# In every step of a local-attention stack, the order of two transposes on TensorE and of four pieces of work on ScalarE is changed

## The reference, cut to what matters

```
for i in range(DEPTH):                                # 6
    x = attn_layer(shift_tokens(x), Wqkv[i], q_scale[i], k_scale[i], Wo[i]) + x
    x = ffn_layer(shift_tokens(x), ln_g[i], ln_b[i], W1[i], b1[i], W2[i], b2[i]) + x

def attn_layer(x, Wqkv, qs, ksc, Wo):                 # HEADS 16, DIM_HEAD 64
    q, k, v = split(x @ Wqkv)
    q, k = l2norm(q) * qs, l2norm(k) * ksc            # needs the inverse lengths of q and k
    q, k = rotary(q), rotary(k)
    out = local_attention(q, k, v)                    # windows of 32 queries see 64 keys; softmax
    return out @ Wo
```

## Time and profile before

| | |
|---|---|
| Median of 3 runs | 4589.51 us (4580.05 to 4589.95) |
| The profiled execution | 4575.15 us |
| Its span, first to last instruction | 4573.3 us |
| Instructions | 164587 |
| TensorE busy | 4055.2 us, 89% |
| GpSimd busy | 3001.9 us, 66% |
| VectorE busy | 2776.7 us, 61% |
| ScalarE busy | 2723.2 us, 60% |

### The profile page before, as it was taken

One profiled execution on the slowest core, in us unless ns is written; L12 is line 12 of the kernel. 1 busy time (PEld: TensorE's weight loads), 2 busy tenths in 40 slices (PEclk: granted clock), 3 DMA queues, 4 the chain that ended last, 5 costly groups with the idle time before them and its releaser, 6 DMA issues.

```text
span 4573.3 us, 164587 instructions
## 1 busy us (share of the span) xinstructions
PE 4055.2 (89%) x67239; PEld 2824.1 (62%) x67239; DVE 2776.7 (61%) x4602; ACT 2723.2 (60%) x5657; POOL 3001.9 (66%) x1858
## 2 busy tenths in 40 slices
PE   8989999999999999967999999999999997276975
PEld 5656666666666666635666666666666663153654
DVE  5556666666666666635666666666666663624541
ACT  5656666666666666634666666666666664134752
POOL 0068888888888888815888888888888882511001
PEclk9999999999999999989999999999999998587997
DMA  2023333333333333312333343333333331030004
GB/s 68 2 65 88 102 98 92 102 91 102 99 92 103 90 101 100 92 39 50 95 99 97 89 107 94 97 98 89 106 94 98 98 89 32 0 111 14 2 11 122
DMA packets 349821, 367.95 MB, mean 80 GB/s; under 512 B 58737, under 2 KB 285042, under 8 KB 348786
## 3 DMA queue, kind: packets, MB, share of 16 engines
q1 hardware_dynamic: 338834, 348.92, 29.2%
q0 software_dynamic: 2048, 4.20, 0.3%
q10 hardware_dynamic: 8160, 3.93, 0.3%
HBM read 247.12 MB, written 109.71 MB: 78 GB/s over the span
## 4 chain that ended last, share of the span: by engine, by line
PE 35%; ACT 8%; issue 3%; POOL 2%; DVE 2%; SPq 1%; DMA 1%; ACTq 0%; POOLq 0%; DVEq 0%
PE banks L325 6%; PE banks L386 3%; PE banks L309 3%; PE banks L330 3%; PE banks L430 2%; PE banks L369 2%; PE banks L292 2%; PE banks L845 1%; PE banks L424 1%; PE banks L863 1%; ACT arena L461 1%; PE banks L880 1%; PE banks L1311 1%; PE banks L1331 1%; ACT ln_rs L467 1%
## 5 line engine op out<-in xcount | busy, mean ns | idle before, releaser
L637 POOL TENSOR_TENSOR arena<-arena 128x512 f32<-128x512 f32 x768 | 960.4, 1272 | 522.6 <-DVE arena L566 401.6
L642 POOL TENSOR_TENSOR arena<-arena 128x1024 f32<-128x1024 f32 x384 | 905.9, 2359 | 30.1
L639 POOL TENSOR_TENSOR arena<-arena 128x1024 f32<-128x1024 f32 x384 | 907.8, 2364 | 0.0
L325 PE MATMUL banks<-w_qk,arena 128*128 128x512 f32 x1536 | 735.7, 602 | 15.5 <-DVE arena L666 10.6
L440 ACT COPY arena<-banks 128x512 f32<-128x512 f32 x384 | 224.3, 584 | 806.1 <-PE banks L386 806.1
L566 DVE SCALAR_TENSOR_TENSOR arena<-arena,banks 128x512 f32<-128x512 f32 x768 | 493.3, 684 | 308.1 <-ACT arena L474 306.6
L559 DVE TENSOR_REDUCE arena<-arena 128x8 f32<-128x512 f32 x768 | 494.2, 679 | 86.4 <-ACT arena L456 86.4
L533 DVE TENSOR_REDUCE arena<-banks 128x8 f32<-128x512 f32 x384 | 264.7, 689 | 399.9 <-PE banks L309 396.2
L456 ACT ACTIVATE arena<-banks 128x512 f32<-128x512 f32 x768 | 447.8, 596 | 82.8 <-PE banks L325 71.0
L325 PEld LDWEIGHTS banks<-w_qk,arena 128*128 128x128 f32 x1536 | 277.0, 193 | 271.6 <-issue 271.6
L386 PE MATMUL banks<-ident,arena 128*128 128x128 f32 x3072 | 424.7, 282 | 20.0 <-POOL arena L642 19.4
(11 more groups left out here) (220 smaller groups left out, 6715.1 us busy)
## 6 DMA issues: line engine op xcount, KB each, us to landing
v_rows<-arena SPq DMA_DIRECT2D x1536, 64.0 KB
arena<-v_rows SPq DMA_DIRECT2D x768, 128.0 KB
arena<-v_rows SPq DMA_DIRECT2D x768, 112.0 KB
arena<-in_moe_w SPq DMA_DIRECT2D x30, 515.5 KB, 3.8
w_qk<-in_stack_qk SPq DMA_DIRECT2D x48, 256.0 KB, 3.1
w_v<-in_stack_v SPq DMA_DIRECT2D x48, 128.0 KB, 3.4
w_o<-in_stack_o SPq DMA_DIRECT2D x12, 512.0 KB
w_w<-in_stack_w SPq DMA_DIRECT2D x12, 341.0 KB, 3.2
```

What stands on the lines that cost most here:

```text
L325: pe.matmul(bank(M, tile), f.sh[:, (s // G) % 2, o:o + 128], w.qk[:, g], start=True, stop=True).then_inc(S.qk, 1)
L637: nc.gpsimd.tensor_tensor(f.sined[:, :, :, half, :], x[:, :, :, 1 - half, :], sines[:, :, mine].unsqueeze(1).to_broadcast([D, GH, 4, DH // ...
L639: nc.gpsimd.tensor_tensor(rot, x.rearrange("p h t a d -> p h t (a d)"), cosines.unsqueeze(1).to_broadcast([D, GH, 4, DH]), ALU.mult).then_ ...
L642: nc.gpsimd.tensor_tensor(rot, rot, f.sined.rearrange("p h t a d -> p h t (a d)"), ALU.add).then_inc(S.rotated, 1)
```

## The change

On TensorE the turning of the outputs, which stood behind the value projection and ahead of place 1, is moved behind place 1 and behind the turning of the probabilities. On ScalarE the order behind the values' copy was outputs' copy, inverse lengths (logarithm, exponential), place 1, probabilities' copy; now it is place 1, probabilities' copy, outputs' copy, inverse lengths, except in steps 3 and 7 (`s % G == 3`), where place 1 stays behind the inverse lengths. The number of instructions and their sizes stay.

```diff
@@ pe_stack_step
-    if st.on(4):
-        u = s - 4
-        st.wait(S.normed, u + 1)
-        st.wait(S.heads_taken, u + 3 if st.on(2) else u + 2 if st.on(3) else u + 1)
-        ...
-        last.then_inc(S.outs_turned, 1)
     pe_stack_hidden(M, st, 1)
-    if st.on(3):
-        ...
-        last.then_inc(S.probs_turned, 1)
+    pe_stack_probs_turned(M, st)
+    pe_stack_outs_turned(M, st)
     if st.on(4) and s % G == 3:
@@ pe_stack_outs_turned (new; holds what was removed above, and one wait for the tail)
+        if not st.on(2):
+            st.wait(S.outs_taken, u)
@@ act_stack_step
     nc.scalar.copy(f.vt[:, u % 2]...).then_inc(S.v_taken, 1)
-    if st.on(4):
-        u = s - 4
-        st.wait(S.outs_turned, u + 1)
-        ...
-        nc.scalar.copy(stack_hidden(M).ot[:, u % G]..., bank(M, 3)).then_inc(S.outs_taken, 1)
+    if s % G != 3:
+        act_stack_hidden(M, st, 1)
+    if st.on(3):
+        u = s - 3
+        st.wait(S.probs_turned, u + 1)
+        st.wait(S.outs, u)
+        nc.scalar.copy(f.pt..., bank(M, 6)).then_inc(S.probs_taken, 1)
+    act_stack_outs(M, st)
     if st.on(0):
         u = s
         st.wait(S.lengths, u + 1)
         nc.scalar.activation(f.lg, f.length, ACT.Ln).then_inc(S.logged, 1)
         ...
         nc.scalar.activation(f.rn[:, u % 2], f.lg, ACT.Exp, scale=-0.5).then_inc(S.inverse, 1)
-    act_stack_hidden(M, st, 1)
-    if st.on(3):
-        ...
-        nc.scalar.copy(f.pt..., bank(M, 6)).then_inc(S.probs_taken, 1)
+    if s % G == 3:
+        act_stack_hidden(M, st, 1)
     act_stack_hidden(M, st, 2)
```

More of the change, by code:

```diff
@@ L332, in pe_stack_step @@
         last.then_inc(S.v, 1)
-    if st.on(4):
-        u = s - 4
-        st.wait(S.normed, u + 1)
-        st.wait(S.heads_taken, u + 3 if st.on(2) else u + 2 if st.on(3) else u + 1)
[L337 to L341, removed]
-        last.then_inc(S.outs_turned, 1)
-    pe_stack_hidden(M, st, 1)
-    if st.on(3):
[L345 to L352, removed]
-        last.then_inc(S.probs_turned, 1)
+    pe_stack_hidden(M, st, 1)
+    pe_stack_probs_turned(M, st)
+    pe_stack_outs_turned(M, st)
     if st.on(4) and s % G == 3:
@@ L372, in pe_stack_step, with pe_stack_outs_turned, pe_stack_probs_turned @@
     pe_stack_hidden(M, st, 2)
+def pe_stack_outs_turned(M, st):
+    pe, s, S, f = st.eng, st.s, M.st, stack_buffers(M)
+    if st.on(4):
+        u = s - 4
+        st.wait(S.normed, u + 1)
+        st.wait(S.heads_taken, u + 3 if st.on(2) else u + 2 if st.on(3) else u + 1)
+        if not st.on(2):
+            st.wait(S.outs_taken, u)
+        ov = f.o.rearrange("p (t h) d -> p t h d", t=2)
+        for hp in range(2):
+            for tile in range(2):
+                last = pe.transpose(bank(M, 3)[:, hp * T + tile * 128:hp * T + tile * 128 + 128],
+                                    ov[:, tile, 2 * hp:2 * hp + 2, :], M.ident[:])
+        last.then_inc(S.outs_turned, 1)
+def pe_stack_probs_turned(M, st):
+    pe, s, S, f = st.eng, st.s, M.st, stack_buffers(M)
+    if st.on(3):
+        u = s - 3
+        st.wait(S.probs, u + 1)
+        st.wait(S.probs_taken, u)
+        pv = f.p.rearrange("p (t h) k -> p t h k", t=2)
+        for tile in range(2):
+            for hp in range(2):
+                o = (2 * tile + hp) * 128
+                last = pe.transpose(bank(M, 6)[:, o:o + 128], pv[:, tile, 2 * hp:2 * hp + 2, :], M.ident[:])
+        last.then_inc(S.probs_turned, 1)
 def pe_stack_heads(M, st, qk):
@@ L457, in act_stack_step @@
                                  ACT.Square).then_inc(S.squared, 1)
+    if st.on(0):
+        u = s
         st.wait(S.v, u + 1)
@@ L461, in act_stack_step @@
         nc.scalar.copy(f.vt[:, u % 2].rearrange("p t a c -> p (t a c)"), bank(M, 2)).then_inc(S.v_taken, 1)
-    if st.on(4):
-        u = s - 4
-        st.wait(S.outs_turned, u + 1)
-        if u % G == 0 and not (st.first and u == 0):
-            act.wait_ge(S.projected, st.f * 2 + u // G)
-        nc.scalar.copy(stack_hidden(M).ot[:, u % G].rearrange("p h t -> p (h t)"), bank(M, 3)).then_inc(S.outs_taken, 1)
+    if s % G != 3:
+        act_stack_hidden(M, st, 1)
+    if st.on(3):
+        u = s - 3
+        st.wait(S.probs_turned, u + 1)
+        st.wait(S.outs, u)
+        nc.scalar.copy(f.pt.rearrange("p t h k -> p (t h k)"), bank(M, 6)).then_inc(S.probs_taken, 1)
+    act_stack_outs(M, st)
     if st.on(0):
@@ L474, in act_stack_step, with act_stack_outs @@
         nc.scalar.activation(f.rn[:, u % 2], f.lg, ACT.Exp, scale=-0.5).then_inc(S.inverse, 1)
-    act_stack_hidden(M, st, 1)
-    if st.on(3):
[L477 to L480, removed]
-    act_stack_hidden(M, st, 2)
+    if s % G == 3:
+        act_stack_hidden(M, st, 1)
+    act_stack_hidden(M, st, 2)
+def act_stack_outs(M, st):
+    act, s, S, nc = st.eng, st.s, M.st, M.nc
+    if st.on(4):
+        u = s - 4
+        st.wait(S.outs_turned, u + 1)
+        if u % G == 0 and not (st.first and u == 0):
+            act.wait_ge(S.projected, st.f * 2 + u // G)
+        nc.scalar.copy(stack_hidden(M).ot[:, u % G].rearrange("p h t -> p (h t)"), bank(M, 3)).then_inc(S.outs_taken, 1)
 def act_stack_hidden(M, st, place):
```

## The result

The changed kernel takes 4635.4 us (median; 4634.11 to 4639.9) against 4588.4 us before, a ratio of 1.0107 with a 95% interval of 1.0092 to 1.0122. It is 47 us slower; 54 were forecast (4643, range 4608 to 4675).

What follows compares the result with a forecast made beforehand. TensorE was taken as the bound, its stops set by ScalarE's order. 36 pairs at +0.97 us and ten layer starts at +2.21 gave 57, taken as 54: 4589.5 + 54 = 4643.5, said as 4643 us, range 4608 to 4675.

Steps and rivals of the forecast that it cites:

- Part 1: Probabilities' copy first on ScalarE: shorter TensorE stops at L309 in steps 0, 5, 6 and at step 6's gate product, at most 1.93 us a pair.
- Step 6: L309's stop and part of the third gate product's wait go, 0.05 us charged for the rotation: -0.87 us.
- Part 2: Outputs' copy one copy later, so L369 waits longer in steps 3 and 7: 2 x 0.48 = 0.96 us a pair.
- Part 3: Inverse lengths (L474) last on ScalarE, delaying VectorE's L566 and the work behind it, and GpSimd's rotation; meets something in four places.
- Step 2 into 3: Inverse lengths delay the next scores' maximum by 1.1 to 1.2 us; about 0.45 reaches L369, ends 0 and 0.8.
- Steps 4 and 5: Inverse lengths 0.54 us late through a chain without slack to the variance, swallowing 0.38 won at L309: +0.54 us.
- Steps 0 and 1: Inverse lengths 1.13 us late stop step 1's value product, leaving 0.11 of L309's 0.63: -0.11 us, +1.13 at layer starts.
- The sum: All terms together: +0.97 us in a usual pair, +2.21 in one starting a later layer; 57 us, taken as 54.
- the late inverse lengths cost nothing: Rival: their delay is hidden in steps 0, 2 and 4, a gain of 0.97 us in 46 pairs, 4545 us; 5%.
- the sum would be nothing: Rival: step 2's delay dies out on the squares and layer starts cost no more than other pairs, near 4595 us; 5%.
- the gains don't come: Rival: L309 and the gate product find another late partner, up to 0.9 us more a pair, about 4680 us; 8%.
- the clock falls in every pair: Rival: longer stops before L369 and in step 5 halve TensorE's clock once a pair, 78 us on top, about 4720; 4%.

## Why the prediction was right, point by point

**What bounds the kernel.** Right. In the pairs TensorE's stops, and who ends them, set the time: every experiment that shortened them shortened the steps. What lies outside the pairs is another matter, as the two runs with step 2 as before show.

**Part 1, the gains.** Right in place and nearly in size. L309 stops no more in steps 0, 5 and 6, and the third gate product has 0.07 left of 0.60. Step 6 won 1.01 in place of 0.87, since the rotation, which I had charged with 0.05, didn't stop it, and the gate product won 0.53 where 0.44 stood.

**Part 2, the later outputs' copy.** Right: 0.96 us in a pair forecast, step 7 grew by 0.48, and undoing it gave 1.0 in a pair back.

**Part 3, the late inverse lengths.** Step 2 into 3: forecast 0.45, and 0.38 of step 3 went when step 2 was undone. The row for the next scores' maximum shows the mechanism; in the changed kernel, VectorE in steps 2 and 3:

```profile
2509.19 1.28 DVE L589 SCALAR_TENSOR_TENSOR arena<-arena,banks 128x512 f32<-128x512 f32 x2 [3.52 <-ACT arena L491]
...
2510.39 0.74 DVE L626 SCALAR_TENSOR_TENSOR z<-banks,w_vecs,z 128x512 f32<-128x512 f32 x1
...
2511.05 0.68 DVE L556 TENSOR_REDUCE arena<-banks 128x8 f32<-128x512 f32 x1
```

The scaling, the state and the maximum follow each other without a gap, where the earlier trace rows have the maximum waiting 1.52 for TensorE. Steps 4 and 5: forecast 0.54, measured 0.71; 0.13 of it is in step 4, where nothing was charged, and it goes when step 4 is undone. Steps 0 and 1: forecast -0.11, measured +0.13. The term that was mis-sized is the delay of 1.13 us. The value projection of step 0 in the trace of before:

```profile
2448.00 1.03 PE L330 MATMUL banks<-w_v,arena 128*128 128x256 f32 x4
```

And in the changed kernel, with the exponential of the inverse lengths:

```profile
2487.82 1.03 PE L330 MATMUL banks<-w_v,arena 128*128 128x256 f32 x4
...
2491.51 0.22 ACT L491 ACTIVATE arena<-arena 128x16 f32<-128x16 f32 x1
```

From the value projection's start to the exponential it is 2.44 before (the exponential at 2450.44 in the earlier trace rows) and 3.69 in the changed kernel, 1.25 more. Another 0.1 is the value product itself: behind its stop it takes 1.12 us (the row at 2493.85) where it took 1.02. At a layer's start step 1 grew from 8.06 to 9.30 us, 1.24 where 1.13 stood.

**The sum.** A usual pair took 1.20 more in place of 0.97, by which the pairs were under-priced by some 10 us. The two stacks' steps took 3366.7 us before and 3437.9 and 3429.3 in the two traces of the changed kernel, 63 to 71 more where I had 57. Those two traces differ by 8.6 us with the same program: TensorE was granted the lower clock for 54 us of the stacks in the one and for 31 in the other (24 before), and its busy time there is 3211.5 and 3203.5 us. Against the growth stand two things that I left out. Between and behind the stacks, with the tails in them, the changed kernel took 4 to 6 us less than before. And the profiled execution of before was a quick one, 5 to 15 us under its other runs, while that of the changed kernel was the slowest of its four: the two spans differ by 65, the medians by 47. So the forecast of 54 for a measured 47 came out close partly by luck: the pairs were priced too low, the tails' gain was missing, and the two misses have opposite signs. That the last stages vary by some 9 us from execution to execution limits how exactly this can be split.

**Rivals.** That the late inverse lengths cost nothing is refuted by the runs with step 0 and step 4 as before. That the sum would be nothing: refuted by the interval. That the gains don't come: refuted by the missing brackets. That the clock falls in every pair: the granted clock of the changed kernel's stacks is 1.00 in the trace shown above and 0.99 in the other, so the projection's stops of up to 1.4 us did not bring it down. It did fall at turns of the hardware loop, where TensorE stands still for 1.9 to 2.5 us and shortly before it for 0.5 to 1.1: at five of the eight turns before, at eight and at six in the two traces of the changed kernel. The warning of the Trainium skill, "TensorE: Matmul & The Clock Gate", "Why this matters for your kernels", about idle gaps between bursts did not come to bear at the projection's stops, and at the turns these traces agree with it.

## What to carry to other kernels

Where several engines pass a tile around in a hand-written order, price a reordering at each place for who waits next, and take it step by step: one order for all eight steps won 1.6 us in a pair and lost 2.8, while choosing per step kept the gains (0.9859, and 0.9709 with the outputs ahead of the values). Work that a third engine is waiting for (here the tiny inverse lengths, 0.2 us each) should not be put behind copies that nobody needs yet. The start and the end of a pipeline run the same code with other neighbours; look at them apart.

## What the runs showed of the hardware

Executions of one kernel differ by as much in stages that no edit touches as a small change is worth. From the second stack's last mask but one to the end, the kernel with step 2 as before took 765.7 us at a granted clock of 0.80 in one trace and 775.3 at 0.78 in the other (the rows above). One trace of each kernel is not enough to lay such a difference to an edit.

The same stop can be followed by the lower clock or not. Seven traces have the old order in step 2 on both engines, and in all their fourteen tails the turning of the outputs waits 2.2 us. In eight of these the three products behind it took 3.8 to 4.4 us, in six, both of the kernel before among them, 2.74. So such a stop, beside other short ones, can cost twice, once itself and once in the products behind it, and whether it does changes between executions of one kernel. The stops of 1.1 to 1.4 us (from start to start) ahead of the projection amid full work, 94 in the changed kernel, never did so inside a pair; there the clock fell only in a stack's first two pairs, behind stops for the rotation (1.78 us before L399 at 337.33).
